# Message passing on one core: a bin's slots summed in PSUM, with the destination of each slot in a register

## The reference

```
edge_index = jnp.stack([src, dst])
# layer 0: h = x @ W.T + b;  out[src] += h[dst]
# layer 1: agg[dst] += h[src];  z = relu(((1+eps)*h + agg) @ W1 + b1) @ W2 + b2;  relu(layernorm(z + h))
# layer 2: agg[src] += edge_weight * x[dst];  two linear maps, each with a batch norm over all nodes and relu
# layer 3: attention: e = concat(h_i, h_j, edge_h) @ a;  softmax over the edges of a target;  out[src] += alpha * h_j
x = _layernorm(x + layer(x))     # after each of them
```

## Time and profile before

| | |
|---|---|
| median of 3 runs | 6711.77 us |
| lowest and highest | 6668.48, 6715.77 us |
| the profiled execution | 6697.6 us, of which the span is 6695.8 us |
| mean granted clock of PE, share of full | 0.735 |
| busy share of the span | PE 55%, DVE 52%, ACT 23%, POOL 60% |
| instructions | 59788 |

### The profile page before, as it was taken

One profiled execution on the slowest core, in us unless ns is written; L12 is line 12 of the kernel. 1 busy time (PEld: TensorE's weight loads), 2 busy tenths in 40 slices (PEclk: granted clock), 3 DMA queues, 4 the chain that ended last, 5 costly groups with the idle time before them and its releaser, 6 DMA issues. The chain is left out here.

```text
span 6695.8 us, 59788 instructions
## 1 busy us (share of the span) xinstructions
PE 3668.7 (55%) x13489; PEld 2668.1 (40%) x13489; DVE 3506.0 (52%) x11201; ACT 1539.5 (23%) x4647; POOL 3992.8 (60%) x4069
## 2 busy tenths in 40 slices
PE   4555555544555555465565545555556455556555
PEld 2343434422333333344444433343443344445444
DVE  5555555544444444455555544444445456666666
ACT  2111111100000000000000012222224345556555
POOL 7666666644666666566666646666661255566553
PEclk8787777765667666677777767777777777777777
DMA  2111111112333333233333323333330223233333
GB/s 82 42 48 43 43 43 46 43 39 67 99 95 99 99 95 99 77 95 98 95 98 96 97 67 92 91 91 92 92 91 27 76 82 85 84 87 90 85 88 60
DMA packets 257644, 522.16 MB, mean 78 GB/s; under 512 B 88394, under 2 KB 128798, under 8 KB 257316
## 3 DMA queue, kind: packets, MB, share of 16 engines
q0 software_dynamic: 179984, 423.92, 22.5%
q1 hardware_dynamic: 77331, 94.66, 4.8%
HBM read 483.72 MB, written 34.57 MB: 77 GB/s over the span
## 5 line engine op out<-in xcount | busy, mean ns | idle before, releaser
L1307 PE MATMUL ps<-ZT,xT 128*128 128x256 f32 x4704 | 1624.6, 502 | 1186.5 <-DVE ACC L1907 816.0
L716 POOL DMA_INDIRECT ZT<-table,meta_dst x1616 | 1551.2, 960 | 1143.9 <-issue 370.6
L716 POOL DMA_INDIRECT ZT<-table,meta_src x1568 | 1485.2, 947 | 874.8 <-issue 375.2
L1907 DVE TENSOR_TENSOR ACC<-ps,ACC 128x256 f32 x2352 | 999.3, 425 | 1522.4 <-remote 799.1
L1307 PEld LDWEIGHTS ps<-ZT,xT 128*128 128x128 f32 x4704 | 1131.8, 253 | 1665.3 <-issue 818.9
L661 POOL DMA_INDIRECT rec_src<-ZT x800 | 863.9, 1080 | 505.8 <-DVE ZT L1829 269.5
L1317 PE MATMUL ps<-ZT,xT 128*128 128x256 f32 x1664 | 587.0, 527 | 464.7 <-issue 461.6
L1317 PEld LDWEIGHTS ps<-ZT,xT 128*128 128x128 f32 x1664 | 446.4, 276 | 590.2 <-issue 486.9
L1823 DVE SCALAR_TENSOR_TENSOR meta_src<-ps,bc 128x256 f32<-128x256 f32 x800 | 291.4, 421 | 608.9 <-remote 488.2
L1260 PE MATMUL ps<-ewW,xT 128*128 128x256 f32 x1600 | 578.3, 464 | 0.0
L1259 PE MATMUL ps<-bias,ones 128*128 128x256 bf16 x800 | 257.4, 322 | 558.8 <-DVE ZT L1829 265.4
(11 more groups left out here) (436 smaller groups left out, 4362.5 us busy)
## 6 DMA issues: line engine op xcount, KB each, us to landing
ACC<-in_edge_attr SPq DMA_DIRECT2D x200, 240.0 KB
ZT<-table,meta_dst POOLq DMA_INDIRECT x1616
ZT<-table,meta_src POOLq DMA_INDIRECT x1568
rec_src<-ZT POOLq DMA_INDIRECT x800
table<-X SPq DMA_DIRECT2D x98, 128.0 KB
table<-ZT SPq DMA_DIRECT2D x49, 128.5 KB
X<-in_x SPq DMA_DIRECT2D x1, 6144.0 KB
table<-z SPq DMA_DIRECT2D x24, 256.0 KB
```

The costliest lines, as they stand in the source:

```text
L716: pool.indirect_dma_start(rows[:, s % depth, 0:width], None, table[layer], bass.IndirectOffsetOnAxis(ap=ids[:, s, 0:1].bitcast(I32), axis= ...
L1307: nc.tensor.matmul(slot_sum(j), sel[:, k % 2, j, :], ring[:, (2 + k) % RG * G + j, 0:D], start=True, stop=True).then_inc(sem["summed"], 1)
L1907: v.tensor_tensor(dst, slot_sum(j), dst, ALU.add).then_inc(sem["added"], 1)
```

## The change

PE sums all 16 slots of a bin in PSUM, and DVE adds two sums for a bin in place of 17. A bin has two places, `halves`: bank b % 2 for the own tile and bank 2 + b % 2 for the other tile. The first slot's matmul opens the first place, its extra matmul (`sel_x`) opens the second. For each other slot the place is read from the table into a register of PE, 0 or 1024 columns on, and added there. At a bin's end a matmul with zeros (bf16, `ones16` by a broadcast column of zeros) closes each place, and the second of them raises `summed`, so that a bin still raises it 17 times: the last slot's own matmul doesn't. PE waits for `added` once for a bin (for the bin two before), no longer at each pair. DVE's `accumulate` runs once for a bin, after its second group: it loads two registers, waits for all 17 increments of the bin, and makes two adds; the second raises `added` by 16. The table `bin_tile` holds the tile's column for the bin's own and other tile and, in the other 15 places, 1024 where the slot's tile isn't that of the bin's first slot and 0 where it is; two operations of DVE make that. The rest is a bf16 tile of zeros and the numbering of a chain of waits on POOL (left out below).

```diff
@@ -250,6 +250,7 @@
         ev = sb("ev", [P, G])
         bias = sb("bias", [P, 2, G])
         mv = sb("mv", [P, KC, 8])
+        zero16 = sb("zero16", [P, 2], BF16)
 
         acc3 = ACC[:, :].rearrange("p (t w) -> p t w", w=D)
         accd = acc3[:, :, 0:D]
@@ -358,7 +359,10 @@
         psf = ps[:, :, :].rearrange("p b c -> p (b c)")
         lane_x = [ends[:, 0, n, :] for n in range(2)]
         node_no = ps[:, 7, 0:P]
-        cross_sum = ps[:, 6, 0:D]
+
+        def bin_sums(b):
+
+            return ps[:, b % 2, 0:D], ps[:, 2 + b % 2, 0:D]
 
         def y_pair(j, i):
 
@@ -615,7 +619,9 @@
+            pool.memset(zero16[:, :], 0.0).then_inc(sem["split_chain"], 1)
+            pool.wait_ge(sem["split_chain"], 1)
...
@@ -1296,16 +1302,29 @@
                 first = 1 if k % 2 == 0 else 0
                 wait(pe, *ring_filled(layer, r, k))
                 wait(pe, sem["sel_ready"], g + (layer * GROUPS + 1))
+                b = bin_of(r, k)
+                halves = bin_sums(b)
+                _, past = nc.values_load_multi_w_load_instructions(
+                    (tile_src, tile_dst, tile_src)[layer][0:1, b * (BIN + 1) + 1 + first + (1 - first) * G:
+                                                          b * (BIN + 1) + 1 + (2 - first) * G],
+                    engines=(mybir.EngineType.PE,), min_val=0, max_val=2 * 512,
+                    skip_runtime_bounds_check_because="a slot's sum goes to one of two halves")
                 if first:
-                    wait(pe, sem["cross_ready"], bin_of(r, k) + (layer * T + 1))
-                    wait(pe, sem["added"], n - BIN)
-                    nc.tensor.matmul(cross_sum, sel_x[:, :], ring[:, (2 + k) % RG * G, 0:D], start=True,
-                                     stop=True).then_inc(sem["summed"], 1)
+                    wait(pe, sem["cross_ready"], b + (layer * T + 1))
+                    wait(pe, sem["added"], layer * SUMS + (b - 1) * (BIN + 1))
+                    nc.tensor.matmul(halves[1], sel_x[:, :], ring[:, (2 + k) % RG * G, 0:D], start=True,
+                                     stop=False).then_inc(sem["summed"], 1)
                 for j in range(G):
-                    if j % 2 == 0:
-                        wait(pe, sem["added"], n + j - (G - 2))
-                    nc.tensor.matmul(slot_sum(j), sel[:, k % 2, j, :], ring[:, (2 + k) % RG * G + j, 0:D],
-                                     start=True, stop=True).then_inc(sem["summed"], 1)
+                    opens = first and j == 0
+                    into = halves[0] if opens else psf[:, bass.ds(past[j - first] + (b % 2) * 512, D)]
+                    mm = nc.tensor.matmul(into, sel[:, k % 2, j, :], ring[:, (2 + k) % RG * G + j, 0:D],
+                                          start=bool(opens), stop=False)
+                    if first or j < G - 1:
+                        mm.then_inc(sem["summed"], 1)
+                if not first:
+                    nothing = zero16[:, 0:1].to_broadcast([P, D])
+                    nc.tensor.matmul(halves[0], ones16[:, :], nothing, start=False, stop=True)
+                    nc.tensor.matmul(halves[1], ones16[:, :], nothing, start=False, stop=True).then_inc(sem["summed"], 1)
 
             def slot_sums_3(g, q, b, e):
                 wait(pe, *ring_filled_3(b, e))
@@ -1316,6 +1335,8 @@
                         wait(pe, sem["added"], n - G + min(2, G - j))
                     nc.tensor.matmul(slot_sum(j), sel[:, q, j, :], ring_3[:, ring_slots_3(e), 0:D][:, j, :],
                                      start=True, stop=True).then_inc(sem["summed"], 1)
+
+            pe.wait_ge(sem["tile_ready"], 2)
 
             def sums_round(r):
                 for k in quarters(r):
@@ -1682,6 +1703,9 @@
                 halves = ((ps[:, 7, 0:25 * BIN], 0, 25), (ps[:, 6, 0:24 * BIN], 25, T))
                 for half, b0, b1 in halves:
                     link(v.tensor_scalar(bin_tile[n][:, b0:b1, 1:], half.rearrange("p (b i) -> p b i", i=BIN), float(D), None, ALU.mult))
+                rest = bin_tile[n][:, :, 2:]
+                link(v.tensor_tensor(rest, rest, bin_tile[n][:, :, 1:2].to_broadcast([P, T, BIN - 1]), ALU.not_equal))
+                link(v.tensor_scalar(rest, rest, float(2 * 512), None, ALU.mult))
                 v.tensor_scalar(bin_tile[n][:, :, 0], ps[:, 6, 400:400 + T], float(D), None, ALU.mult).then_inc(sem["tile_ready"], 1)
                 link(v.tensor_scalar(donor[:, n, 0:T], ps[:, 7, 400:400 + T], lane_no[:, :], None, ALU.is_le))
                 link(v.tensor_copy(table_at[n][:, SLOTS:SUMS], ps[:, 6, 450:450 + T]))
@@ -1891,20 +1915,17 @@
                 return registers(tiles, i * R + k * G, G)
 
             def accumulate(layer, r, k):
-                first = 1 if k % 2 == 0 else 0
-                into = registers((tile_src, tile_dst, tile_src)[layer], sums_until(0, r, k), G + first)
-                n = sums_until(layer, r, k)
-                if first:
-                    dst = ACC[:, bass.ds(into[0], D)]
-                    wait(dve, sem["summed"], n + 1)
-                    wait(dve, sem["added"], n)
-                    v.tensor_tensor(dst, cross_sum, dst, ALU.add).then_inc(sem["added"], 1)
-                for j in range(G):
-                    dst = ACC[:, bass.ds(into[first + j], D)]
-                    if j % 2 == 0:
-                        wait(dve, sem["summed"], n + first + slot_done(j, j))
-                    wait(dve, sem["added"], n + first + j)
-                    v.tensor_tensor(dst, slot_sum(j), dst, ALU.add).then_inc(sem["added"], 1)
+                b = bin_of(r, k)
+                n = layer * SUMS + b * (BIN + 1)
+                other_tile, own_tile = registers((tile_src, tile_dst, tile_src)[layer], b * (BIN + 1), 2)
+                halves = bin_sums(b)
+                dve.wait_ge(sem["summed"], n + BIN + 1)
+                wait(dve, sem["added"], n)
+                dst = ACC[:, bass.ds(own_tile, D)]
+                v.tensor_tensor(dst, halves[0], dst, ALU.add).then_inc(sem["added"], 1)
+                dve.wait_ge(sem["added"], n + 1)
+                dst = ACC[:, bass.ds(other_tile, D)]
+                v.tensor_tensor(dst, halves[1], dst, ALU.add).then_inc(sem["added"], BIN)
 
             def aggregate(layer, r, during):
                 last = isinstance(r, int) and r == ROUNDS - 1
@@ -1915,7 +1936,8 @@
                             select(layer, r, k + 1)
                         else:
                             select(layer, r + 1, 0)
-                    accumulate(layer, r, k)
+                    if k % 2 == 1:
+                        accumulate(layer, r, k)
                     if inside and k in during:
                         during[k](r - 1)
 
```

28 lines of the change are left out of this document (14 added, 14 removed).

## The result

| | before | after |
|---|---|---|
| median of 12 runs | 6698.29 us | 6661.88 us |
| lowest and highest | 6668.48, 6720.36 | 6632.14, 6683.52 |
| the profiled execution | 6697.6 us | 6644.8 us |
| mean granted clock of PE | 0.735 | 0.749 |
| busy share: PE, DVE, ACT, POOL | 55, 52, 23, 60% | 52, 39, 23, 60% |

The ratio of after to before is 0.9938, 95% interval 0.9918 to 0.9958. The change is worth 36 us. Forecast were 195. The time of 6661.88 lies in the range, near its upper end, but nearly all of the expected gain is missing.

A forecast was written before the change was run, and what follows sets the result against it. Gathers at 1.25 us, plus POOL's stops for PE's late increments, were taken to bound three aggregation stages. From 6697.6 us, 150 for fewer stops and 45 for shorter tails gave 6502.6 us; range 6330 to 6710.

The forecast's parts named there:

- What bounds the kernel: Layers 0 to 2: gathers set the pace; POOL stops when PE's `summed` increments come late, 436.3 us of excess.
- The step that failed: POOL's stops in layers 0 to 2: each costs 2.44 us, so fewer stops save 150 us.
- The cycle followed slot by slot: From one POOL stop to the next: 16 or 24 slots, 20 taken, where it was 13.
- The trickle: While POOL issues without a gap, PE's increments of `summed` arrive one in about 5 us; the edit makes it no faster.
- The tails: Last gather to last add in layers 0 to 2: 17 us afterwards, saving 22, 15 and 8 us, 45 in all.
- DVE's adds: 2205 adds fewer, 937 us of DVE's busy time, worth nothing by itself on the path.
- PE's loads: 294 register loads on PE, taken at 2.1 us each, mostly hidden under matmuls; cost taken as 0.
- The clock: PE's groups of eight slots after idle gaps: 8.4 us at the lower clock, still under POOL's 10.0 us.
- The second: Rival: POOL stops as often as now and only the tails are saved, 6653 us; chance 0.22.
- its sign: Mark of the rival with unchanged stops: a stage still takes 1120 us with some 60 waits of POOL.
- The first: Rival: late messages go with the pair hand-overs, POOL never stops, 6216 us; chance 0.15.
- The third: Rival: the bin's message is the chain, deciding from a 10.2 us wait on; slower, 6844 us; chance 0.10.

The follow-up runs named there:

- g8l: Changed kernel with 2 increments of `summed` a bin instead of 17, on a late chip, executed once: 6524.83 us, 0.991 of the kernel before.
- af: The changed kernel itself, unaltered, on a chip that delivers increments at once: 5581.28 us, 1.0012 of the kernel before.
- b2: Kernel before with one increment of `summed` for a pair of slots, 8 a bin instead of 17, on a chip delivering at once: 5569.94 us, 0.9998.
- hb: Kernel before fetching only the even slots (half the gathers) in layers 0 to 2, sums wrong, on a late chip: 5420.89 us.
- ha: Changed kernel fetching only the even slots (half the gathers) in layers 0 to 2, sums wrong, on a late chip: 5021.03 us.
- st: Changed kernel without PE's register loads and register addresses, sums wrong, on a chip delivering at once: 5572.15 us, 1.0001 of the kernel before.
- w2: Changed kernel gathering 512 bytes a row instead of 1024 in layers 0 to 2, sums wrong, on a late chip: 0.9949 of the kernel before.
- p9: Changed kernel with nine small POOL memsets behind each gather of layers 0 to 2, on a late chip: 6616.65 us, 1.0051 of the kernel before.

## Why the prediction was wrong

**What bounds the kernel** held in its first half. The pace is a thing of the gathers, common to the three stages, and POOL stops because PE's increments come late. Chips without late increments have 0 to 8 us of excess in a stage of 784 gathers, with the kernel before's form as well as with the changed one's. (PE's wait of 8.00 us, told as a wait for DVE, stands as "issue" in the earlier trace rows; DVE's adds ended 0.05 us before its end, so the reading holds.)

**The step that failed** is the one from there to a price: "this stop is the 2.44 us that is paid 179 times". The number of stops was taken as what the change can lower and their length as fixed, so 20 slots to a stop in place of 13 saved 150 us; measured are 7.7. g8l did bring them to one per 23 gathers, and they lasted 3.8 to 4.4 us in the mean. The product is what stands still, 0.17 us a gather. Not even the number moved in the kernel after: one stop per 13.4 gathers. The cycle followed slot by slot was sound work on the wrong quantity.

**The trickle** of one increment in 5 us, read from the earlier trace rows, is real, and the kernel after shows it again. But it was read as a capacity for increments. With 2 for a bin the messages were as late as with 17. They are the victims of a backlog, and how many there are is no matter.

It could have been read from the trace of before. The three stages take 1.427 to 1.442 us a gather with quite different work beside them; the text used that to find the common cause, and then gave the excess to stops of even length. Had the stops been set beside the number of gathers since the stop before them, layer 1 would have hinted at it: in POOL's timeline of before the time over 1.25 us a gather is 2.4 to 2.5 us after 12 gathers (four times), 3.0 to 3.7 after 16 (24 times), 3.0 to 3.8 after 20 (four times) and 7.1 after 28 (once), though 4.3 after the first 44. Layers 0 and 2 show it less clearly. No rival had a limit that the gathers themselves run into.

**The tails** went the way that was forecast, by too large a size. Expected were 17 us in each layer, 45 saved; measured 27.5, 19.4 and 21.9, 31.6 saved. The term took PE and DVE to be at most two groups behind at the last gather and left late messages out. Layer 0's tail in the kernel after, in DVE's and PE's timelines:

```profile
2677.26 1.22 DVE L1894 TENSOR_TENSOR xT<-ps,meta_src 128x1024 f32<-128x1024 f32 x1 [21.10 <-remote]
...
2681.48 8.34 PE L1320 MATMUL ps<-ZT,xT 128*128 128x256 f32 x32
...
2690.17 0.43 DVE L1925 TENSOR_TENSOR ACC<-ps,ACC 128x256 f32 x1 [9.20 <-PE ps L1327]
```

PE had closed the bin before the last at 2659.05 and DVE heard of it 18 us later, so that the last bin's matmuls could start only 17 us after the last gather; the last bin's own message, with POOL silent, comes at once. Where nothing is late (af), the tails are 10.6, 8.9 and 10.4 us. There the kernel before's form has the shorter ones (b2: 8.6, 7.9 and 7.7 us). So what the change saves in the tails is late messages as well, and not work of PE and DVE.

**DVE's adds** were taken at nothing on the path, and that held: 922 us less of DVE, and less than 8 us in the stages. hb and ha show what covered them. With half the gathers the three stages take 2176 us with the adds and pairs and 1800 without, on one chip.

**PE's loads** go up to 2.47 us, over the 2.1 taken as the dear end; the median is 1.70. Line 1307 of the kernel after, durations in ns as min/median/max:

```profile
L1307 PEldq TENSOR_LOAD <-tile_src x196: 599/1702/2467, 1557.7 to 5014.7; - x196
```

The Trainium skill ("DMA: Bandwidth & Descriptors", "Latency and other measured facts") puts the floor of such a load at about 600 ns; the shortest here is 599. On chips that deliver at once they are hidden under POOL: without them (st) the time is 1.0001 of before, with them (af, on another chip) 1.0012, intervals that overlap. On a late chip no run left them out.

**The clock.** Had each group of eight slots run at the lower clock throughout, as was weighed, it would take 8.4 us. In the kernel after, groups behind 4 us of idle time and more took 5.1 to 6.8 us, and the one of 1569.67, behind 3.52 us, 3.72; the granted clock in the stages is 0.71, 0.75 and 0.74, a little above. All are under the 10 us of eight gathers, so the clock decided nothing in the stages.

**The rivals.** The second, as many stops as now and only the tails saved, 6653 us, is what happened, by its time and by its sign (59, 56 and 61 waits in stages of 1118 to 1129 us); it had 0.22. That it came so near was luck. Its reason, that selections need every increment of a group, isn't what the runs showed: g8l raises `summed` once for a group, and its stages take as long as w2's with 17 for a bin. The first, POOL never stops, is true on four of the seven chips of the experiments, for both forms of the kernel, and so is worth nothing to the change. The third didn't come: the wait for a bin was up to 37 us, far over its 10.2, but POOL's own limit covers it.

## What to carry to other kernels

When an engine stops for late messages, set the length of each stop beside the work since the last one: if it grows in proportion, the stops may be the draining of a rate limit, and then neither fewer hand-overs nor fewer messages shorten their sum, as neither did here. A change that relieves engines which are idle anyway paid only in the tails here; run it with the bound eased (half the gathers here) to see what it holds in store. And see a kernel on more than one chip before its waits are explained, since this one's late messages weren't there on four of seven.

## What the runs showed of the hardware

- The kernel before takes 5571 to 5580 us on four chips and 6584 to 6698 on the others, with equal durations of gathers (0.95 us) and adds (0.42 us). PE's increments are 0.02 us late there and up to 39 us here. DVE's own increments (`added`) are on record within 0.01 us on both kinds, though on the late chips many of them aren't on record (134 of 294 are, in the kernel after). Behind the late start of layer 0 in the kernel after PE's increments come 4.9 to 5.6 us apart; when POOL stands still before 1612.41, nine of them come within 0.34 us.
- The stages of layers 0 to 2 are less than half of what a late chip costs. The kernel after takes 6643.1 us in its profile and 5587.9 in af's: 414 us of the difference lie in the three stages, 344 before the first gather, 39 in the tails and 260 behind the last add of layer 2. Layer 3's gathers are 1.61 us apart in the mean on the late chip and 1.30 in af, so 1.42 us a gather doesn't account for them; why wasn't looked into.
- On the late chips the limit shows neither in POOL's issues nor in the data: a gather takes 0.95 us, the next can start 1.25 us after it, and the last packet of a gather is done 1.45 us after the end of its issue (the median in the kernel after, in g8l, in p9 and in af's layers 1 and 2 alike; 1.2 with half the bytes in w2). Only PE's increments are seen late. In the edge stage, with scatters of 128 rows of 24 bytes at most, the kernel after's POOL has 64 stops over 1.2 us on the late chip, af none.
- A memset of 16 columns behind a gather costs POOL 0.01 us, four small ones 0.07 and nine 0.19, of the 0.34 us that the nine are busy: the rest lies in the 0.30 us that POOL needs between two gathers anyway.
